# Attention block on one core: how the low halves of the probabilities are shared between VectorE and GpSimd

## The chip, the cores and the metric

One core of a Trainium2 chip runs the whole kernel. The metric is the device time in microseconds (us) of one launch. Engines carry their profile names: PE is TensorE (its matmuls; PEld its weight loads), DVE VectorE, ACT ScalarE, POOL GpSimd, SP the queue that issues the DMAs.

## The reference, cut to what matters

Sixteen images of 32 x 32 positions (1024 tokens) with 512 channels go through group norm, SiLU, one projection to q, k and v, attention with 8 heads of 64 channels, an output projection, a bias and the residual:

```python
xn = jax.nn.silu(group_norm(x, gn_scale, gn_offset))      # x: (16, 32, 32, 512) float32
qkv = jnp.einsum('bxyc,cd->bxyd', xn, w_qkv)
q, k, v = jnp.split(qkv, 3, axis=-1)
...
sim = jnp.einsum('bhdi,bhdj->bhij', q * HEAD_CH ** (-0.5), k)
attn = jax.nn.softmax(sim, axis=-1)
out = jnp.einsum('bhij,bhdj->bhid', attn, v)
out = jnp.einsum('bxyd,dc->bxyc', out, w_out) + b_out
return out + x
```

## The kernel before, in words

Accuracy is kept by splitting each float32 operand into two float16 parts, high and low, and multiplying them in several passes. So every probability exists as `P32` (float32), `Ph` (its float16 high part) and `Pl` (float16 of `P32 - Ph`).

**Units.** Attention of one image is 64 units, written (step, u) with four steps of 16. A unit covers one head, 512 queries and 256 keys. For unit v:

- PE makes the scores in `ST` (two slots, 4 matmuls, lines 1051 and 1052).
- ACT takes the exponential twice: `P32` (line 605, two buffers) and `Ph` (line 608, four buffers, then `exp_done`).
- The low part `Pl = P32 - Ph` is 128 x 1024, cut in two halves: DVE makes columns 0 to 511 (line 812), POOL columns 512 to 1023 (line 495), both as soon as `exp_done` comes.
- Two units later PE multiplies `Ph` and `Pl` with V into `PV` (`times_v`, line 1081). In an even unit that comes right after the scores, in an odd unit at its end.

**Work beside it.** PE also does in each unit a matmul pair into `TP` from which DVE takes the row maxima of scores to come (`mx`, line 759, called max here), and half of a projection job into `SD` (line 949). A job spans an even unit and the odd one after it; at the start of the next even unit ACT writes its high part (not for the "out" jobs) and DVE its low part or result (lines 700, 705, 712), and only then may PE start the next job in `SD`. After every eighth part of the maxima, always in a unit with u % 4 == 1, DVE makes four shifts `ms` (line 729, 128 x 4, inside `top_use` right after the max); PE needs them at the end of that same unit for `TP<-ident,ms` (line 970), and DVE copies that `TP` to `QK2` (line 763) at the start of the next unit, before the job's drain.

**Other side work of DVE and POOL.** For the next image: `turn` (PE transposes x, `("xt", i)`, through an `ST` slot; ACT copies it to `X`), `channel_stats` (bn_stats, line 773), `aggregate`, two chains of tiny operations on 128 x 4 tiles (mean at the start of (1, 0), lines 738 to 744; variance at (1, 4), lines 748 to 755), `newton` on POOL at (1, 5), `coefficients` (DVE, lines 787 to 797, at (1, 7)), and eight `silu` pieces: ACT makes `z` (line 589) and `th` (line 596), DVE multiplies them (line 802, 128 x 512) and casts to float16 (line 805), POOL makes the low part (`low_xn`, line 482). For the output: POOL normalises (`O32`, line 505) after DVE's `sums` (lines 819, 820); `turn` with `("ot", p)` transposes `O32`, ACT copies it, and DVE makes its low part in the next unit (`low_output`, line 721, 128 x 1024); POOL adds the bias (`add_bias`, line 487).

**Order.** Each engine's program is written out by hand: `step` of each engine goes through u = 0 to 15 and looks up in tables of (step, u) what to do after the unit's fixed work. An engine never runs out of this order. Semaphores count; each wait is for a count. The loop holds two images per turn.

Of the kernel before, what the change touches and what calls it, by code (L numbers as in the profile page):

```python
# [10 lines left out]
ALU = mybir.AluOpType  # L11
# [9 lines left out]
HALF = 512  # L21
# [3 lines left out]
UNITS = 64  # L25
# [69 lines left out]
def job_before(step, u, first=False, last=False):  # L95
# [2 lines left out]

TURNS = {(0, 1): ("xt", 0), (0, 3): ("xt", 1), (0, 4): ("ot", 3), (0, 7): ("xt", 2), (0, 9): ("xt", 3),
         (2, 0): ("ot", 0), (2, 8): ("ot", 1), (3, 4): ("ot", 2)}


def unit_turn(step, u, first=False, last=False):
# [11 lines left out]
    return ring  # L117


BN_AT = {(0, 5): (0, 2), (0, 7): (4, 6), (0, 11): (1, 3), (0, 13): (5, 7)}  # L120
AGGREGATE_AT, NEWTON_AT, COEF_AT = (0, 14), (1, 5), (1, 7)
Z_AT = [(1, 8), (1, 11), (1, 13), (2, 1), (2, 4), (2, 7), (2, 11), (2, 13)]
TANH_AT = [(1, 9), (1, 12), (1, 15), (2, 3), (2, 5), (2, 9), (2, 12), (2, 15)]
SILU_AT = [(1, 11), (1, 13), (2, 0), (2, 4), (2, 7), (2, 11), (2, 13), (3, 0)]
LOW_XN_AT = [(1, 12), (1, 14), (2, 1), (2, 5), (2, 8), (2, 12), (2, 14), (3, 1)]
BIAS_AT = {(3, 0): 0, (3, 2): 1, (3, 5): 2, (3, 6): 3}
LATE_BIAS_AT = {(1, 0): 4, (1, 2): 5, (1, 6): 6, (1, 8): 7}


def image_of_tops(b, step, u):  # L130
# [63 lines left out]
def wait(eng, sem, count):  # L194

    if not isinstance(count, int) or count > 0:
        eng.wait_ge(sem, count)


def conv_attention(nc, x, gamma, beta, w_qkv, w_out, b_out, out):  # L200
# [4 lines left out]
    with ctx:  # L205
# [132 lines left out]
        def _(sp):  # L338
# [42 lines left out]
            def step(b, s, cnt, first=False, last=False):  # L381
                for u in range(16):
                    if u % 2 == 0:
                        for use in unit_job(s, u, first, last):
                            cnt.passed(use)
                    if s == 0 and not last:
                        if u == 0 and first:
                            load_x(b + 1, 0)
                        if u in (1, 3, 7):
                            load_x(b + 1, (1, 3, 7).index(u) + 1)  # L390
                    if s == 0 and u == 4:
                        move_v(b)
# [52 lines left out]
        def _(pool):  # L445
# [44 lines left out]
            def low_probs(b, v):  # L490

                pool.wait_ge(exp_done, UNITS * b + v + 1)

                wait(pool, pv_done, UNITS * b + v - 3)
                nc.gpsimd.tensor_tensor(Pl[:, v % 4, HALF:], P32[:, v % 2, HALF:], Ph[:, v % 4, HALF:], ALU.subtract  # L495
                                        ).then_inc(lo_pool, 1)

            def normalise(b, half):
# [11 lines left out]
            def step(b, s, par, first=False, last=False):  # L510
                for u in range(16):
                    v = 16 * s + u
                    if not (first and v == 0):
                        low_probs(b, v - 1)
                    if v % 4 == 3 and not (first and v == 3):
                        normalise(b, v // 4 - 1)
                    if (s, u) == NEWTON_AT and not last:
                        newton(b + 1)
                    if (s, u) in LOW_XN_AT and not last:
                        low_xn(b + 1, 1 - par, LOW_XN_AT.index((s, u)))  # L520
                    if (s, u) in BIAS_AT:
# [30 lines left out]
        def _(act):  # L552
# [46 lines left out]
            def exponentials(b, v, cnt):  # L599
                slot = cnt.next_slot()  # L600
                act.wait_ge(scores_ready, UNITS * b + v + 1)

                wait(act, lo_dve, UNITS * b + v - 1)
                wait(act, lo_pool, UNITS * b + v - 1)
                nc.scalar.activation(P32[:, v % 2, :], ST[:, slot, :], ACT.Exp, scale=cns[:, 0:1])  # L605

                wait(act, pv_done, UNITS * b + v - 3)
                nc.scalar.activation(Ph[:, v % 4, :], ST[:, slot, :], ACT.Exp, scale=cns[:, 0:1]  # L608
                                     ).then_inc(exp_done, 1)
# [60 lines left out]
        def _(dve):  # L670
# [136 lines left out]
            def low_probs(b, v):  # L807

                dve.wait_ge(exp_done, UNITS * b + v + 1)

                wait(dve, pv_done, UNITS * b + v - 3)
                nc.vector.tensor_tensor(Pl[:, v % 4, 0:HALF], P32[:, v % 2, 0:HALF], Ph[:, v % 4, 0:HALF],  # L812
                                        ALU.subtract).then_inc(lo_dve, 1)

            def sums(b, half):

# [6 lines left out]
            def step(b, s, par, cnt, first=False, last=False):  # L823
                turned = []
                for u in range(16):
# [4 lines left out]
                        top_use(use, b + 1, cnt)  # L830
                    for use in job_before(s, u, first, last):
                        side(use, image_of(use, b, s), cnt)
                    for use, slot in turned:
                        low_output(use[1], image_of(use, b, s), slot)
                    if not (first and v == 0):
                        low_probs(b, v - 1)
                    if v % 4 == 3 and not (first and v == 3):
                        sums(b, v // 4 - 1)
                    for use in unit_max(s, u, last):
# [92 lines left out]
            step(B - 2, 3, 0, now)  # L932
            for s in range(4):
                step(B - 1, s, 1, now, last=True)
            low_probs(B - 1, UNITS - 1)
            sums(B - 1, 15)
            low_output(3, B - 1, now.next_slot())
            for t in range(TB):
# [4 lines left out]
        def _(pe):  # L943
# [112 lines left out]
            def times_v(b, v, cnt):  # L1056

                head, kp = v // 8, v % 4
                pe.wait_ge(exp_done, UNITS * b + v + 1)
                if kp == 0:  # L1060

                    wait(pe, pv_out, 16 * b + v // 4)
# [2 lines left out]
                if v == 32:  # L1065
                    pe.wait_ge(v_moved, 16 * (b + 1))
                for i in range(2):
                    pe.wait_ge(lo_pool if i else lo_dve, UNITS * b + v + 1)
                    kb = 2 * kp + i
                    for qb in range(4):  # L1070
                        at, to = i * HALF + qb * P, qb * (LO + HD)
# [107 lines left out]
```

## Time and profile before

| | |
|---|---|
| median of 3 runs | 3912.16 us (3911.99 to 3916.34) |
| the profiled execution | 3913.47 us, its span 3911.7 us |
| PE busy | 3645.2 us, 93% of the span |
| DVE busy | 3350.5 us, 86% |
| ACT busy | 2812.9 us, 72% |
| POOL busy | 1766.6 us, 45% |
| chain that ended last | PE 59%, DVE 24%, issue 12%, ACT 3% |

In the timeline rows, the bracket is the engine's idle time just before the row and what ended it. The busy time of PE is a sum of matmul durations that overlap, so 93% is not a measure of what is left. Steady images follow each other in the middle of the span; image 5's first score matmul starts at 1300.2 us, image 6's at 1535.4 us. Times of the timeline views below are us from the span's start.

### The profile page before, as it was taken

To read this page: it belongs to the slowest core of one execution; us is meant where nothing else is said; L and a number is where in the kernel's file an instruction comes from. 1 tells how busy PE (TensorE), PEld (TensorE's weight loads), DVE (VectorE), ACT (ScalarE), POOL (GpSimd) and SP (SyncE) were. 2 spreads that over 40 slices of the span, in tenths; PEclk is the share of its full clock that TensorE was granted. 3 is DMA by queue.
4 is the path that set the end of the run, shared out by engine and by line. 5 is a ranking of instruction groups with operands and counts; after the bars stand their busy time and mean duration, and the time that the engine had idled before them with its cause. 6 is when DMAs were issued, how large, how long until landed. Compare 5 with 4: busy or idle time off the path is not lost.

```text
span 3911.7 us, 92342 instructions
## 1 busy us (share of the span) xinstructions
PE 3645.2 (93%) x32844; PEld 2099.9 (54%) x32844; DVE 3350.5 (86%) x4368; ACT 2812.9 (72%) x3074; POOL 1766.6 (45%) x1738
## 2 busy tenths in 40 slices
PE   3889999999999999999999999999999999999997
PEld 1455555555555555555555555555555555555553
DVE  5688888988898898988989888898988989888885
ACT  2577677777777777777777777777777777777774
POOL 1244444445445354444445444454444545444443
PEclk7999999999999999999999999999999999999999
DMA  2211212221121321212222121321212222131220
GB/s 77 56 44 51 76 39 66 55 74 52 45 82 34 88 55 45 82 39 66 55 69 58 44 80 36 87 55 45 79 42 66 55 69 58 39 84 37 62 59 33
DMA packets 120727, 228.89 MB, mean 59 GB/s; under 512 B 12624, under 2 KB 29008, under 8 KB 120272
## 3 DMA queue, kind: packets, MB, share of 16 engines
q1 hardware_dynamic: 120272, 222.87, 21.0%
q8 instruction: 279, 4.57, 0.5%
q14 instruction: 176, 1.44, 0.1%
HBM read 71.57 MB, written 33.55 MB: 27 GB/s over the span
## 4 chain that ended last, share of the span: by engine, by line
PE 59%; DVE 24%; issue 12%; ACT 3%; DVEq 1%; DMA 1%; POOL 0%; SPq 0%; ACTq 0%; POOLq 0%
PE SD L949 22%; PE PV L1081 11%; DVE mx L759 8%; PE ST L1051 8%; PE ST L1052 8%; PE TP L963 7%; DVE Pl L812 4%; DVE z L802 3%; DVE ms L729 2%; PE TP L970 2%; PE ST L1016 1%; DVE res L712 1%; PE ST L1023 1%; DVE st L773 1%; DVE OT L721 1%
## 5 line engine op out<-in xcount | busy, mean ns | idle before, releaser
L495 POOL TENSOR_TENSOR Pl<-P,Ph 128x512 f16<-128x512 f32 x1024 | 1240.1, 1211 | 1714.7 <-ACT Ph L608 1705.1
L605 ACT ACTIVATE P<-ST,cns 128x1024 f32<-128x1024 f32 x1024 | 1142.1, 1115 | 896.2 <-PE ST L1052 866.5
L759 DVE TENSOR_REDUCE mx<-TP 128x1 f32<-128x1024 f32 x1024 | 1246.4, 1217 | 165.2 <-PE TP L963 157.4
L608 ACT ACTIVATE Ph<-ST,cns 128x1024 f16<-128x1024 f32 x1024 | 1134.6, 1108 | 0.0
L812 DVE TENSOR_TENSOR Pl<-P,Ph 128x512 f16<-128x512 f32 x1024 | 978.8, 956 | 10.2 <-ACT Ph L608 6.1
L1081 PE MATMUL PV<-V,Ph 128*128 128x129 f16 (+2 forms) x10240 | 862.6, 210 | 4.4 <-POOL Pl L495 1.6
L1081 PEld LDWEIGHTS PV<-V,Ph 128*128 128x128 f16 x10240 | 772.3, 97 | 126.3 <-ACT pv_sum L616 9.2
L1081 PE MATMUL PV<-V,Pl 128*128 128x65 f16 x8192 | 835.2, 192 | 0.0
L1081 PEld LDWEIGHTS PV<-V,Pl 128*128 128x128 f16 x8192 | 723.2, 98 | 108.8 <-issue 0.8
L1051 PE MATMUL ST<-QK 128*128 128x512 f16 x2048 | 778.5, 380 | 0.2 <-ACT Ph L608 0.2
L1052 PE MATMUL ST<-QK 128*128 128x512 f16 x2048 | 778.1, 380 | 0.0
L949 PE MATMUL SD<-X,wq 128*128 128x512 f16 x3072 | 751.4, 381 | 23.6 <-POOL X L482 16.3
L963 PE MATMUL TP<-QK 128*128 128x512 f16 x2048 | 610.7, 380 | 27.1 <-DVE QK L763 14.0
L949 PEld LDWEIGHTS SD<-X,wq 128*128 128x128 f16 x3072 | 293.7, 98 | 406.7 <-DVE QK L700 43.0
L949 PE MATMUL SD<-wo,OT 128*128 128x512 f16 x1536 | 377.1, 383 | 45.5 <-DVE QK L700 28.2
L949 PE MATMUL SD<-wq,X 128*128 128x512 f16 x1536 | 374.3, 381 | 17.0 <-DVE V L705 15.4
L1051 PEld LDWEIGHTS ST<-QK 128*128 128x128 f16 x2048 | 202.9, 99 | 183.7 <-issue 2.5
L1052 PEld LDWEIGHTS ST<-QK 128*128 128x128 f16 x2048 | 200.6, 98 | 182.1 <-issue 2.2
L949 PEld LDWEIGHTS SD<-wo,OT 128*128 128x128 f16 x1536 | 145.9, 98 | 245.8 <-DVE res L712 39.0
L763 DVE CAST QK<-TP 64x512 f16<-64x512 f32 x256 | 176.0, 687 | 116.4 <-PE TP L970 113.7
L700 DVE SCALAR_TENSOR_TENSOR QK<-SD,sc,QK 128x512 f16<-128x512 f32 x256 | 191.4, 748 | 95.8 <-ACT QK L562 80.8
L505 POOL TENSOR_TENSOR O<-pv_sum,den 128x256 f32<-128x256 f32 x256 | 158.1, 617 | 239.0 <-DVE pv_sum L820 237.1
(96 smaller groups left out, 2849.6 us busy)
## 6 DMA issues: line engine op xcount, KB each, us to landing
QK<-QK SPq DMA_DIRECT2D x384, 256.0 KB, 4.7
res<-in_x SPq DMA_DIRECT2D x128, 256.0 KB, 2.8
out<-res SPq DMA_DIRECT2D x128, 256.0 KB, 2.0
x_in<-in_x SPq DMA_DIRECT2D x61, 512.0 KB, 3.8
V<-V SPq DMA_DIRECT2D x16, 1040.0 KB, 6.4
V<-in_L_conv_w_qkv SPq DMA_DIRECT2D x1, 3072.0 KB, 10.7
P<-in_L_conv_w_out SPq DMA_DIRECT2D x1, 1024.0 KB, 12.2
z<-in_x SPq DMA_DIRECT2D x1, 512.0 KB, 6.8
```

The source lines that it names most:

```text
L495: nc.gpsimd.tensor_tensor(Pl[:, v % 4, HALF:], P32[:, v % 2, HALF:], Ph[:, v % 4, HALF:], ALU.subtract).then_inc(lo_pool, 1)
L605: nc.scalar.activation(P32[:, v % 2, :], ST[:, slot, :], ACT.Exp, scale=cns[:, 0:1])
L608: nc.scalar.activation(Ph[:, v % 4, :], ST[:, slot, :], ACT.Exp, scale=cns[:, 0:1]).then_inc(exp_done, 1)
L700: nc.vector.scalar_tensor_tensor(out=QK[:, lo, cols], in0=SD[:], scalar=sc[:, col:col + 1], in1=QK[:, hi, cols], op0=ALU.mult, op1=ALU.sub ...
L759: nc.vector.reduce_max(mx[:, hh, qb:qb + 1], TP[:], AX.X).then_inc(top_drained, 1)
L763: nc.vector.tensor_copy(QK2[r, head_slot(pair, hh), 0, bass.ts(half, HALF)], TP[r, 0:HALF]).then_inc(top_drained, 1)
L812: nc.vector.tensor_tensor(Pl[:, v % 4, 0:HALF], P32[:, v % 2, 0:HALF], Ph[:, v % 4, 0:HALF], ALU.subtract).then_inc(lo_dve, 1)
L949: ins = nc.tensor.matmul(SD[:], stationary(i, c), moving(j, c), start=(c == 0 and i + j == 0), stop=(c == CC - 1 and i == 1))
L963: ins = nc.tensor.matmul(TP[:, bass.ts(kh, HALF)], QK1[:, slot, 0, bass.ts(qb, P)], QK1[:, slot, 1, bass.ts(kh, HALF)], start=True, stop=True)
L1051: nc.tensor.matmul(dst, QK1[:, at, 1, kb], QK1[:, at, 0, bass.ts(q, HALF)], start=True, stop=False)
L1052: ins = nc.tensor.matmul(dst, QK2[:, at, 1, kb], QK2[:, at, 0, bass.ts(q, HALF)], start=False, stop=True)
L1081: ins = nc.tensor.matmul(PV[:, cols], stationary, moving, start=kb == qb == n == 0, stop=kb == TB - 1, skip_group_check=True)
```

## The change

The probabilities' low part is no longer cut in halves. DVE makes it whole (128 x 1024) for even units, POOL whole for odd units. Both still do so while the next unit is being scored: DVE in its odd units, POOL in its even units. The waits follow: the exponential of unit v waits for the low part of unit v - 2 by the engine that makes it, and `times_v` waits once for one engine, ahead of all its matmuls, where it waited for each half. `low_output` comes after the low part on DVE, not before. The tables place side work elsewhere: bn_stats one per unit, SiLU pieces all in odd units, `low_xn` and the bias in even units, the turns of x 2 and 3 at (0, 5) and (0, 7) with their loads to match, the turn of output pair 1 at (2, 12).

```diff
-TURNS = {(0, 1): ("xt", 0), (0, 3): ("xt", 1), (0, 4): ("ot", 3), (0, 7): ("xt", 2), (0, 9): ("xt", 3),
-         (2, 0): ("ot", 0), (2, 8): ("ot", 1), (3, 4): ("ot", 2)}
+TURNS = {(0, 1): ("xt", 0), (0, 3): ("xt", 1), (0, 4): ("ot", 3), (0, 5): ("xt", 2), (0, 7): ("xt", 3),
+         (2, 0): ("ot", 0), (2, 12): ("ot", 1), (3, 4): ("ot", 2)}
...
-SILU_AT = [(1, 11), (1, 13), (2, 0), (2, 4), (2, 7), (2, 11), (2, 13), (3, 0)]
+SILU_AT = [(1, 9), (1, 13), (1, 15), (2, 3), (2, 5), (2, 9), (2, 11), (2, 15)]
...
-LATE_BIAS_AT = {(1, 0): 4, (1, 2): 5, (1, 6): 6, (1, 8): 7}
+LATE_BIAS_AT = {(1, 0): 4, (1, 2): 5, (1, 4): 6, (1, 6): 7}
...
 POOL, low_probs and step:
-                nc.gpsimd.tensor_tensor(Pl[:, v % 4, HALF:], P32[:, v % 2, HALF:], Ph[:, v % 4, HALF:], ALU.subtract
+                nc.gpsimd.tensor_tensor(Pl[:, v % 4, :], P32[:, v % 2, :], Ph[:, v % 4, :], ALU.subtract
                                         ).then_inc(lo_pool, 1)
...
-                    if not (first and v == 0):
+                    if v % 2 == 0 and not (first and v == 0):
                         low_probs(b, v - 1)
...
 ACT, exponentials:
-                wait(act, lo_dve, UNITS * b + v - 1)
-                wait(act, lo_pool, UNITS * b + v - 1)
+                wait(act, lo_pool if v % 2 else lo_dve, 32 * b + v // 2)
...
 DVE, low_probs and step:
-                nc.vector.tensor_tensor(Pl[:, v % 4, 0:HALF], P32[:, v % 2, 0:HALF], Ph[:, v % 4, 0:HALF],
-                                        ALU.subtract).then_inc(lo_dve, 1)
+                nc.vector.tensor_tensor(Pl[:, v % 4, :], P32[:, v % 2, :], Ph[:, v % 4, :], ALU.subtract
+                                        ).then_inc(lo_dve, 1)
...
+                    if v % 2 == 1:
+                        low_probs(b, v - 1)
                     for use, slot in turned:
                         low_output(use[1], image_of(use, b, s), slot)
-                    if not (first and v == 0):
-                        low_probs(b, v - 1)
...
 PE, times_v:
                 pe.wait_ge(exp_done, UNITS * b + v + 1)
+                pe.wait_ge(lo_pool if v % 2 else lo_dve, 32 * b + v // 2 + 1)
...
-                    pe.wait_ge(lo_pool if i else lo_dve, UNITS * b + v + 1)
```

The first place is DVE's order around the output turn of unit (3, 4), rows of register arithmetic left out. Before:

```order
L700 SCALAR_TENSOR_TENSOR QK<-SD,sc,QK 128x512
L812 TENSOR_TENSOR Pl<-P,Ph 128x512
L759 TENSOR_REDUCE mx<-TP 128x1
L721 TENSOR_TENSOR OT<-ST,OT 128x1024
L812 TENSOR_TENSOR Pl<-P,Ph 128x512
L759 TENSOR_REDUCE mx<-TP 128x1
L729 TENSOR_SCALAR ms<-mx,cns 128x4
```

The same place on DVE with the change:

```order
L700 SCALAR_TENSOR_TENSOR QK<-SD,sc,QK 128x512
L759 TENSOR_REDUCE mx<-TP 128x1
L812 TENSOR_TENSOR Pl<-P,Ph 128x1024
L721 TENSOR_TENSOR OT<-ST,OT 128x1024
L759 TENSOR_REDUCE mx<-TP 128x1
L729 TENSOR_SCALAR ms<-mx,cns 128x4
```

Between the max of unit (3, 4) and the one of (3, 5) stood 1024 + 512 columns of work; now 1024 + 1024, with the half ahead of the first max gone.

The second place is DVE's order in units (2, 4) and (2, 5), with the start of (2, 6), around one SiLU piece (`z` and `X`). Before:

```order
L812 TENSOR_TENSOR Pl<-P,Ph 128x512
L759 TENSOR_REDUCE mx<-TP 128x1
L802 SCALAR_TENSOR_TENSOR z<-th,z 128x512
L805 CAST X<-z 128x512
L812 TENSOR_TENSOR Pl<-P,Ph 128x512
L759 TENSOR_REDUCE mx<-TP 128x1
L729 TENSOR_SCALAR ms<-mx,cns 128x4
L763 CAST QK<-TP 64x512
L700 SCALAR_TENSOR_TENSOR QK<-SD,sc,QK 128x512
```

The same units on DVE with the change:

```order
L759 TENSOR_REDUCE mx<-TP 128x1
L812 TENSOR_TENSOR Pl<-P,Ph 128x1024
L759 TENSOR_REDUCE mx<-TP 128x1
L729 TENSOR_SCALAR ms<-mx,cns 128x4
L802 SCALAR_TENSOR_TENSOR z<-th,z 128x512
L805 CAST X<-z 128x512
L763 CAST QK<-TP 64x512
L700 SCALAR_TENSOR_TENSOR QK<-SD,sc,QK 128x512
```

The SiLU piece stood ahead of the shifts `ms`; now it stands behind them, and ahead of the copy of `TP` and the drain of the job.

## Rows read from the trace of the kernel before

**Rows 1.** The page, part 1: busy time and share of each engine.

```profile
PE 3645.2 (93%) x32844; PEld 2099.9 (54%) x32844; DVE 3350.5 (86%) x4368; ACT 2812.9 (72%) x3074; POOL 1766.6 (45%) x1738
```

**Rows 2.** Waits of PE: engine, line, releaser: us in total, times, longest us.

```profile
PE TP L970 <- DVE ms L729: 98.1, 98, 3.0
PE SD L949 <- DVE QK L700: 36.5, 18, 3.4
...
PE SD L949 <- DVE V L705: 15.4, 36, 1.6
PE SD L949 <- DVE res L712: 14.8, 49, 0.8
PE TP L963 <- DVE QK L763: 14.0, 30, 2.1
```

**Rows 3.** Groups by line: busy us, mean ns; then idle before and releasers.

```profile
L495 POOL TENSOR_TENSOR Pl<-P,Ph 128x512 f16<-128x512 f32 x1024 | 1240.1, 1211 | 1714.7 <-ACT Ph L608 1705.1 <-PE PV L1081 6.5 <-POOL gn L476 3.1
L812 DVE TENSOR_TENSOR Pl<-P,Ph 128x512 f16<-128x512 f32 x1024 | 978.8, 956 | 10.2 <-ACT Ph L608 6.1 <-DVE mv L779 2.7 <-issue 0.7
...
L505 POOL TENSOR_TENSOR O<-pv_sum,den 128x256 f32<-128x256 f32 x256 | 158.1, 617 | 239.0 <-DVE pv_sum L820 237.1 <-PE PV L1081 1.9
```

**Rows 4.** Timeline, SiLU piece at (1, 13): start, duration, engine, operation [idle before].

```profile
1409.91 0.69 DVE L802 SCALAR_TENSOR_TENSOR z<-th,z 128x512 f32<-128x512 f32 x1
1410.63 1.26 DVE L805 CAST X<-z 128x512 f16<-128x512 f32 x1
...
1410.18 1.43 POOL L495 TENSOR_TENSOR Pl<-P,Ph 128x512 f16<-128x512 f32 x1 [2.48 <-ACT Ph L608]
...
1412.67 0.61 PE L963 MATMUL TP<-QK 128*128 128x512 f16 x2 [0.41 <-DVE QK L763]
1413.46 1.25 PE L949 MATMUL SD<-wo,OT 128*128 128x512 f16 x5 [0.18 <-DVE res L712]
```

**Rows 5.** Timeline, image 5, end of unit (0, 1).

```profile
1306.85 1.16 POOL L495 TENSOR_TENSOR Pl<-P,Ph 128x512 f16<-128x512 f32 x1 [1.48 <-ACT Ph L608]
1307.14 0.89 DVE L729 TENSOR_SCALAR ms<-mx,cns 128x4 f16<-128x4 f32 x1
1308.09 0.40 PE L970 MATMUL TP<-ident,ms 128*128 128x128 f16 x4 [0.24 <-DVE ms L729]
```

**Rows 6.** Timeline, image 5, units (3, 4) and (3, 5), which hold an output turn.

```profile
1497.15 1.23 DVE L759 TENSOR_REDUCE mx<-TP 128x1 f32<-128x1024 f32 x1 [1.22 <-PE TP L963]
1498.29 1.21 DVE L721 TENSOR_TENSOR OT<-ST,OT 128x1024 f16<-128x1024 f32 x1
...
1500.20 1.21 DVE L759 TENSOR_REDUCE mx<-TP 128x1 f32<-128x1024 f32 x1
1501.44 0.23 DVE L729 TENSOR_SCALAR ms<-mx,cns 128x4 f16<-128x4 f32 x1
...
1501.51 1.18 POOL L495 TENSOR_TENSOR Pl<-P,Ph 128x512 f16<-128x512 f32 x1 [1.78 <-ACT Ph L608]
...
1501.73 0.40 PE L970 MATMUL TP<-ident,ms 128*128 128x128 f16 x4
```

**Rows 7.** The page, part 6: a DMA issue, count, KB each, us to landing.

```profile
x_in<-in_x SPq DMA_DIRECT2D x61, 512.0 KB, 3.8
```

**Rows 8.** Timeline, image 5, unit (2, 5), PE, after a SiLU piece in (2, 4).

```profile
1441.80 0.28 PE L970 MATMUL TP<-ident,ms 128*128 128x128 f16 x2 [1.47 <-DVE ms L729]
```

**Rows 9.** Timeline, image 5, starts of units (1, 0) and (1, 4), DVE and POOL.

```profile
1360.78 1.20 DVE L742 TENSOR_TENSOR gn<-gn 128x4 f32<-128x4 f32 x1
...
1360.69 1.27 POOL L487 TENSOR_TENSOR res<-res,bias 128x512 f32<-128x512 f32 x1
...
1374.11 0.55 DVE L751 TENSOR_SCALAR gn<-gn 128x4 f32<-128x4 f32 x1
...
1373.48 1.16 POOL L495 TENSOR_TENSOR Pl<-P,Ph 128x512 f16<-128x512 f32 x1 [0.75 <-ACT Ph L608]
```

**Rows 10.** Timeline, image 5, unit (1, 8), PE, behind the coefficients of (1, 7).

```profile
1391.74 0.82 PE L949 MATMUL SD<-wo,OT 128*128 128x512 f16 x3 [2.19 <-DVE QK L700]
```

More of the change, by code:

```diff
@@ L117, in ring_of @@
     return ring
-BN_AT = {(0, 5): (0, 2), (0, 7): (4, 6), (0, 11): (1, 3), (0, 13): (5, 7)}
+BN_AT = {(0, 5): (0,), (0, 6): (2,), (0, 7): (4,), (0, 8): (6,), (0, 9): (1,), (0, 10): (3,), (0, 12): (5,),
+         (0, 13): (7,)}
 AGGREGATE_AT, NEWTON_AT, COEF_AT = (0, 14), (1, 5), (1, 7)
-Z_AT = [(1, 8), (1, 11), (1, 13), (2, 1), (2, 4), (2, 7), (2, 11), (2, 13)]
-TANH_AT = [(1, 9), (1, 12), (1, 15), (2, 3), (2, 5), (2, 9), (2, 12), (2, 15)]
-SILU_AT = [(1, 11), (1, 13), (2, 0), (2, 4), (2, 7), (2, 11), (2, 13), (3, 0)]
-LOW_XN_AT = [(1, 12), (1, 14), (2, 1), (2, 5), (2, 8), (2, 12), (2, 14), (3, 1)]
-BIAS_AT = {(3, 0): 0, (3, 2): 1, (3, 5): 2, (3, 6): 3}
-LATE_BIAS_AT = {(1, 0): 4, (1, 2): 5, (1, 6): 6, (1, 8): 7}
+Z_AT = [(1, 7), (1, 9), (1, 12), (1, 15), (2, 3), (2, 5), (2, 8), (2, 11)]
+TANH_AT = [(1, 8), (1, 11), (1, 13), (2, 1), (2, 4), (2, 7), (2, 9), (2, 13)]
+SILU_AT = [(1, 9), (1, 13), (1, 15), (2, 3), (2, 5), (2, 9), (2, 11), (2, 15)]
+LOW_XN_AT = [(1, 10), (1, 14), (2, 0), (2, 4), (2, 6), (2, 10), (2, 12), (3, 0)]
+BIAS_AT = {(3, 2): 0, (3, 6): 1, (3, 8): 2, (3, 10): 3}
+LATE_BIAS_AT = {(1, 0): 4, (1, 2): 5, (1, 4): 6, (1, 6): 7}
 def image_of_tops(b, step, u):
@@ L388, in step @@
                             load_x(b + 1, 0)
-                        if u in (1, 3, 7):
-                            load_x(b + 1, (1, 3, 7).index(u) + 1)
+                        if u in (1, 3, 5):
+                            load_x(b + 1, (1, 3, 5).index(u) + 1)
                     if s == 0 and u == 4:
@@ L934, in _ @@
                 step(B - 1, s, 1, now, last=True)
-            low_probs(B - 1, UNITS - 1)
             sums(B - 1, 15)
```

## The prediction

> **What bounds the kernel now.** The page comes first: PE is busy 93% of the span, DVE 86%, POOL 45% [rows 1]. PE is the engine to keep fed; DVE has little to spare. Next the waits of PE [rows 2]: almost all it loses in the steady part it loses to DVE. The five rows add up to 178.8 us (98.1 + 36.5 + 15.4 + 14.8 + 14.0), about 11.5 us in each of the 15 or 16 images. That is what the change can win at most; the other 3.7 ms is PE's own work and the prologue. More than half is one wait, PE for the four shifts `ms`.
>
> Then the groups and the timelines say why DVE is late. The mean of DVE's half of `Pl` is 956 ns [rows 3]. Where nothing disturbs it the same shape takes 0.68 us: the SiLU product, also 128 x 512 with two inputs from SBUF, took 0.69 us [rows 4]. The rest is waiting for POOL inside the instruction. [Rows 5] show it bare: `ms`, four columns, takes 0.89 us instead of 0.23 us [rows 6] because POOL's `Pl` started 0.29 us ahead of it; it ends at 1308.03, 0.02 us after POOL does. [Rows 4] show it both ways: POOL's `Pl` starts at 1410.18 inside the SiLU product, takes 1.43 instead of 1.16 us, and the cast behind the product, 0.03 us late, lies until 1411.89, 0.28 us after POOL's end at 1411.61. So the one that comes first holds SBUF for its whole instruction, and a waiting POOL instruction slips in between two of DVE. The maxima and the drains read PSUM and do not wait (1.21 to 1.23 us in [rows 6], whatever POOL does).
>
> **Durations after the change.** POOL: 256 columns take 0.617 us [rows 3], 512 take 1.16 [rows 5]; another 512 cost 1.08, so a whole unit takes 2.24 us. DVE: 128 x 1024 took 1.21 us in `OT` [rows 6], and the low part has the same width; two halves cost 2 x 0.956. DVE's busy time thus falls by 512 x (1.91 - 1.21) = 360 us, some 23 us an image, and POOL's hardly moves. But PE waits for DVE only at certain places, so the sum is made there.
>
> The Trainium skill (VectorE: DVE Perf Modes, section on the TRN2 errata) says that operations reading SBUF pay their latency once per instruction, so few large ones beat many small ones. The rows agree on the size (2 x 0.68 - 1.21 = 0.15 us a pair); by that rule alone the sum would be a gain of 512 x 0.15 = 77 us if DVE were the bound, against the loss found below.
>
> **Regular units.** A pair of units takes 235.2 / 32 = 7.3 us on average (images 5 to 6). In it DVE has two maxima, a drain of about 0.7 us and its `Pl`, 2 x 1.22 + 0.7 + 1.21 = 4.4 us; POOL's `Pl` with a bias or `low_xn` behind it (1.27 us in [rows 9]) takes 2.24 + 1.27 = 3.5. The one comes in the odd unit, the other from the odd unit's `exp_done` on, so they miss each other. Nothing is lost, but hardly anything was lost there before. PE reads an odd unit's `Pl` only at the end of the odd unit two later, so POOL's longer instruction is hidden there; likewise ACT's wait for `P32`. The earlier turns of x still stand two units after the one before, 7.3 us, against 3.8 us for their load [rows 7]; `move_v`, queued behind the load, was there before. All at nothing. The price is that whatever of DVE falls behind POOL's start now lies 1.08 us longer. In us per image:
>
> *1. Shifts `ms` behind POOL's start.* In a unit with u % 4 == 1 the shifts come ahead of POOL's `Pl` (in [rows 4] even the product behind them does, by 0.27 us), unless something delays the max. At (0, 1) the turn of x does (it stands between scores and max, and POOL waits only for the scores): `ms` is already blocked [rows 5] and will be for 1.08 us more. At (0, 5) there is now a turn of x too; as [rows 5], 0.24 + 1.08 = 1.3. At (3, 5), [rows 6]: max at 1497.15, now the whole `Pl` (1498.29), `OT` (1499.42), the next max (1500.55), `ms` at 1501.79. POOL starts at 1501.51. Before, `ms` passed it by 0.07 us; now it misses by 0.28 and ends at 1503.78, and PE's `TP` comes at 1503.83 in place of 1501.73: +2.1. Sum 4.5.
>
> *2. The other output turns*, (2, 1) and (2, 13), have the same chain, but the SiLU piece before holds PE and with it POOL's start back by about the missing 0.3 us. Even odds on 2.2 each: 2.2. Bounds 0 and 4.4.
>
> *3. SiLU pieces.* All eight are now in odd units, after the max, so POOL's `Pl` slips in between product and cast as in [rows 4]. There PE lost 0.41 + 0.18 by these rows, which show a matmul's end some 0.15 us late, so 0.9 in all; a cast 1.08 us later makes it 1.9 to 2.0. Four pieces stand where a copy of `TP` follows (u % 4 == 1): 4 x 1.9 = 7.6. Two stand at u % 4 == 3 with no turn after, 1.4 each; two have a turn of about 0.9 us after them, 0.5 each. Sum 11.4. Gone are three pieces in even units, which made the next `ms` late: one costs 1.47 [rows 8], and such places make up most of the 98.1 us, 6.1 per image [rows 2]; gone too are the five old odd pieces, 2.7. So 11.4 - 8.8 = +2.6. Bounds 0 (POOL's start falls behind the cast) and 5.
>
> *4. Tiny operations.* At (1, 0) `L742` already waits for POOL's bias [rows 9]; both POOL instructions now hold it to 1.1 us later. The max behind it comes too late for the next `TP` (0.7), and the shifts of (1, 1) then fall behind POOL's `Pl` (1.5): 2.2. At (1, 4) `L751` waits for the end of `Pl` [rows 9], now 1.1 us later, and the bias now placed at (1, 4) may take a further 1.2 in front of the next two; the drain and PE's `SD` wait for them: 1.7. At (1, 7) ACT's first `z` now stands ahead of unit 8's high part and waits for the coefficients; its 0.8 us and what hangs on it add 1.0 to the 2.19 of [rows 10]. Sum 4.9, bounds 2 and 7.
>
> *5. Gone with the smoother order*: one turn of x at (0, 9), bn_stats in pairs, small drains: -1.2.
>
> Sum 4.5 + 2.2 + 2.6 + 4.9 - 1.2 = **+13.0 us an image**. Side work for a next image runs 15 times: 195 us. The profiled execution took 3913.5 us (1.3 above the median), so 3913.5 + 195 = 4108.
>
> **Rivals.** *A (0.13): DVE is the real bound, and the change is faster.* For it: DVE's 86% and its 24% of the chain, and the 360 us of DVE time that go. It decides if casts and shifts mostly find POOL off SBUF, so that terms 1 to 4 vanish and half to all of the 178.8 us goes: 3735 to 3825, say 3815. Against it: [rows 4] is the very order that all eight pieces get.
>
> *B (0.15): POOL's longer instruction lets DVE in midway.* No row shows a POOL instruction above 512 columns on SBUF from which DVE's wait could be read. Then the blocked ones lose no more than today; left are +1.0 at (3, 5), about 1 at (2, 1) and (2, 13), +1 at (1, 8), 2 in term 3: +4 an image, 3975. The Trainium skill (SBUF — State Buffer, section "two separate sides") speaks against B: the pair of ports is locked for the full instruction.
>
> *C (0.04): it is hidden.* Gains of even SiLU pieces (6.1) cancel the losses: 3910.
>
> **How the numbers follow.** My forecast has 0.68. Its own bounds: terms at their low ends give +4, at their high ends +20, 3975 to 4210. About 0.2% is what a measurement can tell from no change. Faster is A, 0.13; same is C, 0.04; slower is the forecast and B, 0.83. The range takes in B and most of the forecast's bounds and leaves A out: 3930 to 4190.
>
> **What would show it.** Right: POOL's `Pl` at 2.24 us, DVE's at 1.21 and mostly undisturbed; `ms` of over 2 us at (0, 1), (0, 5) and (3, 5); casts `X<-z` at about 2.3 us in all odd units; PE's wait for `ms`, `QK` L763 and the drains up from 179 to some 370 us; DVE's busy time down all the same, by less than 360. Wrong: if `ms` stays near 0.23 us in the (3, 5) units, or the casts at 0.43 us, or if PE's waits for DVE shrink.

## The result, and the profile after

The changed kernel takes **4165.66 us** (median of 4 runs, 4164.22 to 4167.66); the kernel before, run beside it, takes 3913.01 us. The ratio is 1.0644, with a 95% interval of 1.0626 to 1.0663: 253 us slower. The forecast was 4108 us, 195 us slower.

The page of the changed kernel, part 1 and the first line of part 4, answering to [rows 1]:

```profile
PE 3696.1 (89%) x32844; PEld 2112.8 (51%) x32844; DVE 3303.4 (79%) x3856; ACT 2819.4 (68%) x3074; POOL 1619.4 (39%) x1226
...
PE 45%; issue 22%; DVE 14%; POOL 7%; ACT 5%; DMA 1%; DVEq 0%; POOLq 0%; SPq 0%; ACTq 0%
```

Every engine but PE is busy for less time or the same, and the kernel is slower. That is what a loss by waiting looks like. POOL now stands in the chain with 7%; before, it had 0%.

The waits of PE, answering to [rows 2] (us in total, times, longest):

```profile
PE TP L969 <- DVE ms L729: 162.3, 86, 2.9
PE SD L948 <- DVE QK L700: 84.5, 48, 3.1
PE TP L962 <- DVE QK L763: 77.7, 59, 2.1
PE SD L948 <- DVE V L705: 22.1, 21, 1.6
PE ST L1015 <- DVE OT L721: 19.9, 14, 1.4
...
PE SD L948 <- DVE res L712: 8.4, 21, 0.8
```

The five waits that made 178.8 us before make 355.0 now (162.3 + 84.5 + 77.7 + 22.1 + 8.4), 176 more. A wait of 19.9 us, the turn of x behind the output's low part, is new. PE's busy time grew by 51 us at the same number of matmuls, most of it because part of them ran at a lower granted clock (below). 176 + 20 + 51 = 247 of the 250.7 us by which the span grew. Busy and waiting time can be added up here: the page counts matmuls that overlap only once, so PE's busy and idle time make up the span (3645.2 + 266.5 before, 3696.1 + 466.3 after). The text ahead of the prediction takes the 93% for a sum of overlapping durations, which it is not.

The 250.7 us are spread over the images: image 5 to image 6 is 1379.05 to 1630.95 us, 251.9 in place of 235.2; the mean of images 3 to 12 grew by 16.2 us, and the last image, which prepares no next one, still by 11.

The groups, answering to [rows 3]:

```profile
L496 POOL TENSOR_TENSOR Pl<-P,Ph 128x1024 f16<-128x1024 f32 x512 | 1101.1, 2151 | 1427.6 <-ACT Ph L608 1426.2 <-issue 1.2
L812 DVE TENSOR_TENSOR Pl<-P,Ph 128x1024 f16<-128x1024 f32 x512 | 623.0, 1217 | 15.7 <-ACT Ph L608 9.3 <-DVE mv L779 2.7 <-issue 1.9
```

The same groups before and after for the two operations that pay; before:

```profile
L729 DVE TENSOR_SCALAR ms<-mx,cns 128x4 f16<-128x4 f32 x256 | 116.3, 454 | 9.1
...
L805 DVE CAST X<-z 128x512 f16<-128x512 f32 x128 | 115.9, 906 | 4.4
```

after:

```profile
L805 DVE CAST X<-z 128x512 f16<-128x512 f32 x128 | 264.5, 2066 | 4.4
...
L729 DVE TENSOR_SCALAR ms<-mx,cns 128x4 f16<-128x4 f32 x256 | 198.1, 774 | 9.1
```

DVE saved 978.8 - 623.0 = 356 us on `Pl`, as counted. But the casts and the shifts took back 149 + 82 of it as waiting inside the instruction, the statistics more, and its busy time fell by 47 us only.

Unit (3, 4) to (3, 5) of image 5, the place of [rows 6] (timeline: start, duration, engine, operation, idle before):

```profile
1591.82 1.22 DVE L812 TENSOR_TENSOR Pl<-P,Ph 128x1024 f16<-128x1024 f32 x1
1592.95 1.22 DVE L721 TENSOR_TENSOR OT<-ST,OT 128x1024 f16<-128x1024 f32 x1
1594.09 1.21 DVE L759 TENSOR_REDUCE mx<-TP 128x1 f32<-128x1024 f32 x1
1595.34 1.84 DVE L729 TENSOR_SCALAR ms<-mx,cns 128x4 f16<-128x4 f32 x1
...
1595.04 2.12 POOL L496 TENSOR_TENSOR Pl<-P,Ph 128x1024 f16<-128x1024 f32 x1 [5.33 <-ACT Ph L608]
...
1597.24 0.40 PE L969 MATMUL TP<-ident,ms 128*128 128x128 f16 x4 [2.00 <-DVE ms L729]
```

`ms` missed POOL's start by 0.30 us (forecast: 0.28), lay until 1597.18, 0.02 us after POOL's end, and PE idled 2.00 us. Unit (1, 13) to (1, 14), the place of [rows 4]:

```profile
1497.41 0.68 DVE L802 SCALAR_TENSOR_TENSOR z<-th,z 128x512 f32<-128x512 f32 x1
1498.13 2.24 DVE L805 CAST X<-z 128x512 f16<-128x512 f32 x1
...
1497.78 2.30 POOL L496 TENSOR_TENSOR Pl<-P,Ph 128x1024 f16<-128x1024 f32 x1 [4.47 <-ACT Ph L608]
...
1501.15 0.60 PE L962 MATMUL TP<-QK 128*128 128x512 f16 x2 [1.37 <-DVE QK L763]
```

The cast takes 2.24 us (forecast: about 2.3) and PE's copy of `TP` comes late.

### The profile page after: what moved, and what is told of

Read it like the earlier page. It is cut to its first block, busy times and chain, and to the rows that moved or that the text cites. A ratio compares the mean times of both kernels' runs of the same rounds, so it can differ in the third digit from the quotient of the medians.

```text
span 4162.4 us, 89409 instructions
## 1 busy us (share of the span) xinstructions
PE 3696.1 (89%) x32844; PEld 2112.8 (51%) x32844; DVE 3303.4 (79%) x3856; ACT 2819.4 (68%) x3074; POOL 1619.4 (39%) x1226
## 4 chain that ended last, share of the span: by engine, by line
PE 45%; issue 22%; DVE 14%; POOL 7%; ACT 5%; DMA 1%; DVEq 0%; POOLq 0%; SPq 0%; ACTq 0%
PE SD L948 17%; PE PV L1080 8%; PE TP L962 6%; PE ST L1051 6%; PE ST L1050 6%; POOL Pl L496 4%; DVE mx L759 4%; DVE ms L729 3%; ACT Ph L608 2%; DVE OT L721 2%; ACT OT L583 1%; PE ST L1015 1%; PE TP L969 1%; POOL res L488 1%; DMA QK<-QK 1%
## 5 line engine op out<-in xcount | busy, mean ns | idle before, releaser
L496 POOL TENSOR_TENSOR Pl<-P,Ph 128x1024 f16<-128x1024 f32 x512 | 1101.1, 2151 | 1427.6 <-ACT Ph L608 1426.2
L962 PE MATMUL TP<-QK 128*128 128x512 f16 x2048 | 619.0, 384 | 91.7 <-DVE QK L763 77.7
L812 DVE TENSOR_TENSOR Pl<-P,Ph 128x1024 f16<-128x1024 f32 x512 | 623.0, 1217 | 15.7 <-ACT Ph L608 9.3
L948 PE MATMUL SD<-wo,OT 128*128 128x512 f16 x1536 | 386.1, 390 | 48.7 <-DVE QK L700 37.8
L962 PEld LDWEIGHTS TP<-QK 128*128 128x128 f16 x2048 | 163.1, 98 | 219.5 <-DVE QK L763 45.5
```

The source lines that it names most:

```text
L496: nc.gpsimd.tensor_tensor(Pl[:, v % 4, :], P32[:, v % 2, :], Ph[:, v % 4, :], ALU.subtract).then_inc(lo_pool, 1)
L812: nc.vector.tensor_tensor(Pl[:, v % 4, :], P32[:, v % 2, :], Ph[:, v % 4, :], ALU.subtract).then_inc(lo_dve, 1)
L948: ins = nc.tensor.matmul(SD[:], stationary(i, c), moving(j, c), start=(c == 0 and i + j == 0), stop=(c == CC - 1 and i == 1))
L962: ins = nc.tensor.matmul(TP[:, bass.ts(kh, HALF)], QK1[:, slot, 0, bass.ts(qb, P)], QK1[:, slot, 1, bass.ts(kh, HALF)], start=True, stop=True)
```

## The terms, unit by unit

The mean time from one unit's first score matmul to the next unit's, over images 3 to 12, in us. An undisturbed unit with u % 4 == 1 takes 3.5, any other undisturbed one 3.3, with a turn 4.17.

| unit | before | after | what is in it |
|---|---|---|---|
| (0, 1) | 4.81 | 5.78 | `ms` behind POOL's start, both times |
| (0, 5) | 3.55 | 6.04 | a turn of x moved in (0.9), and 1.6 of waiting |
| (3, 5) | 3.71 | 5.70 | `ms` behind POOL's start, now |
| (2, 1) | 4.84 | 5.74 | before: SiLU piece in (2, 0); now `ms` blocked |
| (2, 13) | 3.62 | 5.70 | `ms` blocked |
| (1, 1) | 3.61 | 5.70 | `ms` blocked, behind the mean's tiny operations |
| (1, 4) | 3.43 | 5.14 | the variance's tiny operations |
| (1, 8) + (1, 9) | 9.17 | 11.35 | the coefficients and ACT's first `z` |
| (1, 10), (1, 14) | 3.30, 4.23 | 4.90, 5.20 | after a SiLU piece, (1, 14) both times |
| (2, 2), (2, 14) | 3.30, 4.23 | 3.96, 3.79 | now 4.95 in the images in which PE's clock falls there, 3.30 in the others |

## The experiments

All are measured against 3911 to 3914 us for the kernel before, run on the same chip beside them. Each but the last is one execution, so a few us between two of them say nothing. The savings are against the 4165.66 us of the changed kernel.

**Turns and loads moved to even units** (`e1_turns`). The changed kernel with this alone:

```diff
-TURNS = {(0, 1): ("xt", 0), (0, 3): ("xt", 1), (0, 4): ("ot", 3), (0, 5): ("xt", 2), (0, 7): ("xt", 3),
-         (2, 0): ("ot", 0), (2, 12): ("ot", 1), (3, 4): ("ot", 2)}
+TURNS = {(0, 0): ("xt", 0), (0, 2): ("xt", 1), (0, 4): ("xt", 2), (0, 6): ("ot", 3), (0, 8): ("xt", 3),
+         (2, 2): ("ot", 0), (2, 6): ("ot", 1), (3, 6): ("ot", 2)}
-BN_AT = {(0, 5): (0,), (0, 6): (2,), (0, 7): (4,), (0, 8): (6,), (0, 9): (1,), (0, 10): (3,), (0, 12): (5,),
-         (0, 13): (7,)}
+BN_AT = {(0, 3): (0, 2), (0, 5): (4,), (0, 9): (6,), (0, 11): (1, 3), (0, 12): (5,), (0, 13): (7,)}
-                        if u in (1, 3, 5):
+                        if u in (0, 2, 4):
```

> The changed kernel with all turns moved so that none stands in or ahead of a unit with shifts in an odd place: x turns at (0, 0), (0, 2), (0, 4), (0, 8), output turns at (0, 6), (2, 2), (2, 6), (3, 6), loads and bn_stats to match. Theory (shifts fall behind POOL's whole-unit low part): the waits for ms at (0, 1), (0, 5), (2, 1), (2, 13) and (3, 5), about 9.6 us an image, go: 4166 - 150 = about 4015 us. Rival (DVE's longer instruction alone makes it late, wherever the turns stand): about 4166, at most 30 us less.

Measured: 4026.61 us, 139 less than the changed kernel. The wait for `ms`:

```profile
PE TP L968 <- DVE ms L728: 48.9, 26, 3.1
```

From 162.3 to 48.9 us, and from 86 times to 26: four of the five places per image are gone, the fifth, (1, 1), has no turn. So at these four what makes `ms` late is the turn ahead of it, and each wait was worth 113.4 / 60 = 1.9 us. The 19.9 us of the turn of x behind the output's low part are gone too.

**SiLU pieces where POOL is off SBUF** (`e2_silus`). The pieces go to the start of an odd unit with u % 4 == 3, ahead of the max (one, at (2, 13), stays behind the max):

```diff
-SILU_AT = [(1, 9), (1, 13), (1, 15), (2, 3), (2, 5), (2, 9), (2, 11), (2, 15)]
+SILU_AT = [(1, 11), (1, 15), (2, 3), (2, 7), (2, 11), (2, 13), (2, 15), (3, 3)]
...
+                    if (s, u) in SILU_AT and u % 4 == 3 and not last:
+                        silu(b + 1, 1 - par, SILU_AT.index((s, u)))
```

(`Z_AT`, `TANH_AT` and `LOW_XN_AT` move along; the first `z` is at (1, 8) instead of (1, 7), and `low_xn` follows in the same odd unit, but for the piece at (2, 13).)

> The changed kernel with seven SiLU pieces in units with u % 4 == 3 ahead of the max, where POOL is off SBUF, and one left at (2, 13). Theory: product and cast take 0.68 and 0.43 us there and PE's waits behind them, about 9.4 us an image, shrink to about 2: 4166 - 110 = about 4055 us. Rival (the SiLU piece costs PE its own 1.1 us of DVE wherever it stands): within 30 us of 4166.

Measured: 3986.06 us, 180 less than the changed kernel, and 69 less than expected. The cast's group:

```profile
L805 DVE CAST X<-z 128x512 f16<-128x512 f32 x128 | 85.8, 671 | 4.4
```

It takes 671 ns on average in place of 2066. That is not quite undisturbed: seven of the eight casts take 0.72 us, 0.3 of it behind POOL's short `O` instruction (line 506), and the one after (2, 13) takes 0.43. The 180 us are 12.0 an image. Most of what comes on top of the expected gain is not the pieces': units (1, 8) and (1, 9) take 4.55 + 3.52 = 8.07 us in place of 11.35, since ACT's first `z` no longer waits for the coefficients at (1, 7). That leaves 12.0 - 3.3 = 8.7 us for the eight pieces.

**Statistics moved** (`e3_stats`). The mean's tiny operations after the max of (1, 2), the variance's after that of (1, 4), the coefficients at (1, 6), one late bias piece elsewhere:

```diff
-AGGREGATE_AT, NEWTON_AT, COEF_AT = (0, 14), (1, 5), (1, 7)
+AGGREGATE_AT, NEWTON_AT, COEF_AT = (0, 14), (1, 5), (1, 6)
-LATE_BIAS_AT = {(1, 0): 4, (1, 2): 5, (1, 4): 6, (1, 6): 7}
+LATE_BIAS_AT = {(1, 0): 4, (1, 2): 5, (1, 4): 6, (1, 8): 7}
...
+                        if (s, u) == (1, 2):
+                            mean_rest()
+                        if (s, u) == (1, 4):
+                            var_rest()
```

> The changed kernel with the tiny operations of mean and variance put off until after the max of (1, 2) and (1, 4), and the coefficients at (1, 6). Theory: the waits at (1, 0), (1, 1), (1, 4), (1, 8) and (1, 9), about 8.5 us an image with the slower PE clock after the long one, go: 4166 - 120 = about 4045 us, and the granted clock stays at 1.00 in steady images. Rival (tiny operations cost their dependent latencies, not POOL's lock): no more than 30 us less.

Measured: 4049.77 us, 116 less. Thus thirteen operations on 128 x 4 (of fifteen; the two that read PSUM stayed), with what waits for them, cost 7.7 us an image where they stood. Some 3.3 of it is ACT's first `z`, below, which finds its coefficients ready here.

**POOL's low part in two instructions** (`e4_pooltwo`) **and in four** (`e9_poolfour`). Nothing else is changed: same tables, same share, same order.

```diff
-                nc.gpsimd.tensor_tensor(Pl[:, v % 4, :], P32[:, v % 2, :], Ph[:, v % 4, :], ALU.subtract
-                                        ).then_inc(lo_pool, 1)
+                for i in range(4):
+                    cols = bass.ts(i, HALF // 2)
+                    part = nc.gpsimd.tensor_tensor(Pl[:, v % 4, cols], P32[:, v % 2, cols], Ph[:, v % 4, cols],
+                                                   ALU.subtract)
+                part.then_inc(lo_pool, 1)
```

> The changed kernel with POOL's whole-unit low part issued as two instructions of 512 columns back to back. Theory (SBUF is held for one instruction, whatever its length): a waiting DVE instruction gets in between the two, blocked ms and casts end about 1.1 us earlier, 12 to 14 places an image: about 3985 us. Rival (the POOL queue keeps SBUF from instruction to instruction, or DVE is late for its own length): 4166 or slightly more, as POOL gets 0.1 us longer.

> The changed kernel with POOL's whole-unit low part in four instructions of 256 columns, tables of the change. Theory (a DVE instruction waits for the one POOL instruction under way): from one piece to two each blocked ms or cast came about 1.0 us earlier, 4166 to 3954 us; from two to four it comes about 0.5 us earlier again where PE still waits: 3850 to 3890 us, though POOL is 0.3 us longer per unit. Rival (what two pieces gained was a lucky alignment): 3954 us or more.

Measured: 3954.36 us with two (some 30 less than expected), 3887.11 with four (as expected), against 4165.66 with one. The same `ms` of unit (3, 5) that took 1.84 us above, in the kernel with two:

```profile
1511.33 1.15 POOL L496 TENSOR_TENSOR Pl<-P,Ph 128x512 f16<-128x512 f32 x1 [5.19 <-ACT Ph L610]
1511.63 0.87 DVE L731 TENSOR_SCALAR ms<-mx,cns 128x4 f16<-128x4 f32 x1
1512.44 1.15 POOL L498 TENSOR_TENSOR Pl<-P,Ph 128x512 f16<-128x512 f32 x1
...
1512.57 0.40 PE L971 MATMUL TP<-ident,ms 128*128 128x128 f16 x4 [1.04 <-DVE ms L731]
```

and with four (the first row merges three of the four pieces):

```profile
1483.95 1.92 POOL L498 TENSOR_TENSOR Pl<-P,Ph 128x256 f16<-128x256 f32 x3 [4.90 <-ACT Ph L611]
1484.25 0.39 DVE L732 TENSOR_SCALAR ms<-mx,cns 128x4 f16<-128x4 f32 x1
...
1484.70 0.40 PE L972 MATMUL TP<-ident,ms 128*128 128x128 f16 x4 [0.55 <-DVE ms L732]
```

`ms` starts 0.30 us behind POOL's start in all three, and ends when POOL's first instruction does: 1.84, 0.87, 0.39 us. PE waits 2.00, 1.04, 0.55. So SBUF is held for one instruction, not for the whole series, and a waiting DVE instruction gets in between two POOL instructions that stand back to back. That settles the cause: POOL's work even grew (1619.4 to 1858.1 us busy), and the kernel is 278 us faster. What is left is small: 3887.11 is 25 us above the 3861.76 of the halves with the same tables (`e6_newtables`, next). It agrees with the Trainium skill (SBUF — State Buffer, section "two separate sides"), by which the pair of ports is held for the whole instruction.

**Whole units with the old tables** (`e5_oldtables`) **and halves with the new tables** (`e6_newtables`). The two parts of the change, each alone: the first takes `low_probs`, its waits and its order from the change and all tables and the load units from the kernel before; the second the reverse. The first differs from the change by its tables, of which these two show the manner; the second by the halves, which come back as they stand with a minus in the diff of the change:

```diff
-SILU_AT = [(1, 9), (1, 13), (1, 15), (2, 3), (2, 5), (2, 9), (2, 11), (2, 15)]
+SILU_AT = [(1, 11), (1, 13), (2, 0), (2, 4), (2, 7), (2, 11), (2, 13), (3, 0)]
-BIAS_AT = {(3, 2): 0, (3, 6): 1, (3, 8): 2, (3, 10): 3}
+BIAS_AT = {(3, 0): 0, (3, 2): 1, (3, 5): 2, (3, 6): 3}
```

> The changed kernel (whole units by turns, low part ahead of the output's low part on DVE) with all tables of the kernel before. Theory (the loss is the length for which POOL now holds SBUF; the tables only choose where it strikes): the SiLU pieces in even units, the turns at (0, 9) and (2, 8) and the chain at (1, 0) lose as much as the new places do: 4130 to 4190 us. Rival (the loss comes from the new tables): near 3913 us.

> The kernel before (halves, POOL holds SBUF for 1.16 us) with all tables of the change. Theory: near the kernel before, 3900 to 3960 us; shifts and casts blocked at the same places, but for 1.1 us less each; the first z at (1, 7) still costs some 2 us an image. Rival (the tables are the loss): above 4050 us.

| | tables of before | tables of the change |
|---|---|---|
| halves | 3913 | 3861.76 |
| whole units | 4206.31 | 4166 |

The first came out a little above what was expected, the second well below. Whole units cost 293 us in the one column and 304 in the other; the tables gain 51 and 40. The wait for `ms` in the kernel with whole units and old tables, and then in the one with halves and new tables:

```profile
PE TP L968 <- DVE ms L728: 265.4, 143, 3.1
```

```profile
PE TP L971 <- DVE ms L730: 24.1, 27, 3.0
```

That the tables are a gain by themselves was expected neither here nor in the prediction. With halves, the SiLU pieces behind the max in odd units make their casts wait for a 1.16 us instruction, and free `ms` (98.1 us of waiting before, 24.1 now).

**ACT's first `z` one unit later** (`e11b_firstz`). The changed kernel with this alone:

```diff
-Z_AT = [(1, 7), (1, 9), (1, 12), (1, 15), (2, 3), (2, 5), (2, 8), (2, 11)]
+Z_AT = [(1, 8), (1, 9), (1, 12), (1, 15), (2, 3), (2, 5), (2, 8), (2, 11)]
```

(and in each unit ACT makes `z` ahead of `th`, since both fall in (1, 8).)

> The changed kernel with ACT's first z piece at (1, 8), behind the job's high part and the exponentials and ahead of the first th piece, instead of (1, 7). Theory (the first z waits for the coefficients and holds up the high part that PE's next job waits for; the long wait then costs PE its faster clock for a while): units (1, 8) and (1, 9) take 8.1 to 8.5 us together instead of 11.35 and the granted clock there stays at 1.00: 4166 - 48 = about 4118 us. Rival (DVE's coefficients are the wait, whoever needs them): within 15 us of 4166.

Measured: 4118.25 us, 47 less. The windows view over units (1, 8) and (1, 9) of image 5 (us, busy time and count of each engine, PEclk, DMA share, GB/s), in this kernel:

```profile
1456.61:1464.67 8.06, 6.98 (x69) 3.89 (x67) 7.39 (x10) 6.43 (x8) 2.34 (x2) 1.00 0.43 89
```

in the changed kernel, with its two units apart and together:

```profile
1471.60:1478.47 6.87, 4.17 (x36) 1.95 (x34) 5.17 (x7) 4.10 (x5) 2.10 (x1) 0.90 0.11 23
1478.47:1482.97 4.50, 4.50 (x35) 2.34 (x34) 2.40 (x4) 2.56 (x3) 0.36 (x1) 0.78 0.94 210
1471.60:1482.97 11.37, 8.67 (x69) 4.29 (x67) 7.57 (x10) 6.65 (x8) 2.46 (x2) 0.85 0.44 97
```

The same 69 matmuls are busy for 8.67 us in place of 6.98, at a granted clock of 0.85 in place of 1.00. So 3.3 us hang on one ACT instruction per image, 1.7 of them by the clock.

**All three placements together** (`e7_all3`), **and with POOL's low part in two** (`e8_all3two`). Edits as in the first three experiments, and as above.

> The changed kernel with the moves of e1, e2 and e3 together: turns, SiLU pieces and statistics all placed where POOL is off SBUF. Theory: what is left is PE's own 221 us an image, some 2 us behind the one SiLU piece left at (2, 13) and some 1.5 us of small waits: 4166 - 27 x 15.5 = about 3750 us, faster than both kernels. Rival (DVE at its limit; the three gains overlap): above 3850 us.

> e7 with POOL's low part in two instructions. Theory: only the piece at (2, 13) still falls behind POOL, so at most 1 us an image less, 15 us, against POOL's 0.1 us more: 3735 to 3755 us.

Measured: 3798.26 and 3777.62 us, 48 and some 30 more than expected. The three alone add up to 139 + 180 + 116 = 435 us, of which about 50 (3.3 an image) are counted twice, since both the second and the third clear (1, 8): 385 against the measured 367. Most of the rest is (2, 14): the one piece left behind the max, at (2, 13), still has its cast blocked (2.24 us) and costs 1.9 us an image there, where the second experiment alone lost less. Another 0.7 each are left at (2, 4) and (2, 8), behind units that hold both an output's low part and a SiLU piece. Splitting POOL's instruction now gains 21 us where it gained 211 before the moves: the two remedies pay for the same waits.

**Halves with the moved tables** (`e10_halves_all3`, and again, timed in five runs, as `e12_halves_timed`). The kernel before's halves, waits and order of `low_probs`, with the turns, pieces and statistics of the three experiments. Against the three placements together:

```diff
-                nc.gpsimd.tensor_tensor(Pl[:, v % 4, :], P32[:, v % 2, :], Ph[:, v % 4, :], ALU.subtract
+                nc.gpsimd.tensor_tensor(Pl[:, v % 4, HALF:], P32[:, v % 2, HALF:], Ph[:, v % 4, HALF:], ALU.subtract
                                         ).then_inc(lo_pool, 1)
...
-                    if v % 2 == 0 and not (first and v == 0):
+                    if not (first and v == 0):
                         low_probs(b, v - 1)
```

> The kernel before, each low part in halves on both engines, with the tables of the change and the moves of e1, e2 and e3. Theory: with the side work placed off POOL, halves lose only what each half waits for the other, which the order absorbs: 3770 to 3820 us, about as e7 (3798). Rival (whole units by turns are needed for these places to work): above 3850 us, near e6 (3862).

> The kernel of e10 again, timed: 3750 to 3756 us, 4% faster than the kernel before.

Measured: 3752.56 us in one run, below the range expected; **3754.51 us** as the median of 5 runs (3752.22 to 3756.24), with 3913.77 before. The ratio to the kernel before is 0.9595, interval 0.9582 to 0.9609. Its page and its wait for `ms`:

```profile
PE 3610.9 (96%) x32844; PEld 2098.6 (56%) x32844; DVE 3223.5 (86%) x4368; ACT 2813.6 (75%) x3074; POOL 1756.0 (47%) x1738
```

```profile
PE TP L988 <- DVE ms L729: 14.6, 10, 2.5
```

It beats both kernels, and it beats the best one with whole units, by 44 us (by 23 that with two POOL instructions). DVE is busy 290 us more than in the whole-unit kernel with the same placement (2933.8 us) and the kernel is faster: DVE's busy time was not the bound.

## Why the prediction was right and where it was wrong

**The direction, the mechanism and most places were right.** The one that comes first holds SBUF, and what falls behind POOL's start lies as much longer as POOL's instruction is longer. POOL's `Pl` took 2.13 us (2.24 forecast), DVE's 1.22 (1.21), the casts 2.07 on average, 2.2 to 2.4 where they are blocked (2.3). The five waits of PE were to reach some 370 us and reached 355. Two signs failed in size: `ms` was to take over 2 us at (0, 1), (0, 5) and (3, 5) and took 1.86, 0.23 and 1.84, and POOL's busy time, which was hardly to move, fell by 147 us.

**Rival A** (DVE the real bound, 3815) fell. DVE's busy time did go down and the time went up; the halves beat the whole units at every set of tables. The rule on few large operations that was weighed there (the Trainium skill, VectorE: DVE Perf Modes, section on the TRN2 errata) holds for the size: 1217 ns against 2 x 0.68 us. But it speaks of one engine by itself; here the 77 us that it promises stand beside a loss of 293 to 304.

**Rival B** (DVE gets in midway, 3975) fell: the rows with one, two and four pieces show each wait ending with a POOL instruction, never inside one. **Rival C** (hidden, 3910) fell with the result.

**The terms**, in us per image; the measured ones come from the unit table:

| step | forecast | measured |
|---|---|---|
| 1 shifts behind POOL's start | 4.5 | 4.6 |
| 2 the other output turns | 2.2 | 4.4 |
| 3 SiLU pieces | +2.6 | about +1.0 |
| 4 tiny operations | 4.9 | 6.0 |
| 5 gone with the smoother order | -1.2 | -1.4 |
| not in the prediction: small losses, mostly PE's clock | 0 | +1.7 |
| sum | +13.0 | +16.2 |

*Step 1* was right in sum, but at (0, 5) by another way. There `ms` was not blocked:

```profile
1400.95 1.22 DVE L721 TENSOR_TENSOR OT<-ST,OT 128x1024 f16<-128x1024 f32 x1
...
1405.04 0.23 DVE L729 TENSOR_SCALAR ms<-mx,cns 128x4 f16<-128x4 f32 x1
```

PE's turn of x at (0, 5) waited 1.4 us for the low part of the output turned at (0, 4), which DVE now makes after its whole `Pl`; this is the new row of 19.9 us. POOL started as always, 3.3 us into the unit, and `ms` came so late that POOL was all but done:

```profile
1402.22 1.09 PE L1015 MATMUL ST<-ident,x_in 128*128 128x128 f32 x8 [1.42 <-DVE OT L721]
...
1403.03 2.13 POOL L496 TENSOR_TENSOR Pl<-P,Ph 128x1024 f16<-128x1024 f32 x1 [6.21 <-ACT Ph L608]
```

The prediction saw that the two turns now stand in neighbouring units and did not follow the slot from one to the other. That its 1.3 is near the measured 1.6 at (0, 5) is luck: either way `ms` ends at about POOL's end.

*Step 2 is the largest mistake.* It gave even odds to (2, 1) and (2, 13), because a SiLU piece ahead would hold POOL's start back by the missing 0.3 us. Both take 5.7 us on the mean of ten images, against 3.5 undisturbed: 2.2 each. The piece did hold PE and POOL back, by about 0.23 us, which was not enough: `ms` missed POOL's start by 0.05 to 0.07 us there, against 0.30 at (3, 5), and lost all the same. At (2, 1) of image 5:

```profile
1514.20 2.12 POOL L496 TENSOR_TENSOR Pl<-P,Ph 128x1024 f16<-128x1024 f32 x1 [4.05 <-ACT Ph L608]
...
1514.27 2.08 DVE L729 TENSOR_SCALAR ms<-mx,cns 128x4 f16<-128x4 f32 x1
```

The upper bound, 4.4, was the right value.

*Step 3* was sized too high. It charged 11.4 us to the eight pieces; the eight units that follow one take 37.65 us together, less 8 x 3.3 and two turns of 0.87 in them 9.5, and the second experiment gives 8.7. What they replaced was forecast at 8.8 and is some 8.5 by the same count (1.2 of it at (2, 9), behind the old output turn of (2, 8) and not a piece).

*Step 4*: (1, 1) 2.1 (2.2 forecast) and (1, 4) 1.7 (1.7) are as worked out. (1, 8) + (1, 9) lost 2.2, not 1.0. The step saw that ACT's first `z` waits for the coefficients ahead of the high part; the wait grew by 0.5 us only (2.19 to 2.70), and the 1.7 that PE's lower clock costs there was not in the step. Without it the pair takes 8.06 us, 1.1 less than before, so this one entry of a table cost 3.3 an image, 47 us in all by its own run.

*Step 5* was right in size: (0, 9), its turn left out, (0, 14), (0, 6), (1, 2) and some smaller ones gained 1.4 together. What the prediction had nothing for is +1.7 of new small losses. 1.15 of it is at (2, 2) and (2, 14), the units after a blocked `ms`: these take 4.95 us in the images in which PE's clock falls there and 3.30 in the others (last section).

Together 2.2 + 1.1 + 1.7 too little and 1.6 too much, less 0.2 of gain in step 5, make the 3.2 us an image that are missing in images 3 to 12, some 46 us over the 15 images. The last image's 11 us come on top: the prediction counted 15 images, but the last one has shifts and output turns too. Since these errors partly cancel, the sum is nearer to the result than its terms are. Its lower bound was added up wrong as well: the terms at their low ends give 4.5 + 0 + 0 + 2 - 1.2 = +5.3, not +4.

What the prediction didn't ask is whether the two halves of the change have the same sign. They don't: the tables gain 40 to 51 us and whole units lose 293 to 304.

## What to carry to other kernels

Between two engines that exclude each other, the length of one instruction is the price that the other pays for coming second, however small its own work; so keep the instructions of the engine with slack short, even if that engine's busy time grows. Then ask of each operation that reads and writes SBUF which engine comes first there, and move it to a place where the other is off: that was worth 160 us here with the halves left as they were, while cutting the instruction count on DVE lost 293. A change made of a new split and new tables should be costed as two changes, since one can hide the gain of the other.

## What was not expected of the hardware

*The hold is per instruction, with a fine grain.* POOL's two-input float32 subtraction takes 2.13 us for 1024 columns, 1.15 for 512 and 0.67 for 256, and DVE's four-column operation behind it scales with that (1.84, 0.87, 0.39 us). A series of four hides almost all of it.

*A late coefficient lowered PE's clock.* In the changed kernel, PE at (1, 7) and after:

```profile
1471.60 0.38 PE L1050 MATMUL ST<-QK 128*128 128x512 f16 x1
1471.81 0.38 PE L1051 MATMUL ST<-QK 128*128 128x512 f16 x1
...
1476.46 2.21 PE L948 MATMUL SD<-wo,OT 128*128 128x512 f16 x6 [2.70 <-DVE QK L700]
1478.46 0.63 PE L1050 MATMUL ST<-QK 128*128 128x512 f16 x1
1478.89 0.63 PE L1051 MATMUL ST<-QK 128*128 128x512 f16 x1
```

Matmuls of 512 columns follow each other every 0.21 us before (2.4 GHz) and every 0.43 us after (1.2 GHz), behind an idle time of 2.70 us. The granted clock of (1, 9) is 0.78 here and 0.75 and 0.70 one and two images later; over (1, 8) and (1, 9) together it is 0.85 in all three, and the clock falls there in each of images 1 to 14. With the first `z` moved, PE waits 1.08 us there and the clock stays at 1.00 in all of them. So a wait can cost more than its length.

The length of the wait alone does not decide it. Before, the same place waited 1.8 to 2.2 us (2.19 in [rows 10]), and the clock stayed up in all but two of these 14 images. Images 3 and 9 of the kernel before, over (1, 8) and (1, 9), with waits of 2.19 and 2.18 us:

```profile
916.60:925.78 9.18, 6.99 (x70) 3.90 (x68) 7.72 (x14) 5.76 (x7) 3.79 (x5) 1.00 0.38 79
2328.42:2339.27 10.85, 8.67 (x70) 4.32 (x68) 7.73 (x14) 5.77 (x7) 3.77 (x5) 0.84 0.46 103
```

And in the changed kernel (2, 2) runs at the lower clock for a part in 6 of the 14 images, (2, 14) in 3, behind the waits of 2.0 to 2.1 us for `ms`. Unit (2, 2) of images 4 and 5:

```profile
1264.39:1269.33 4.94, 4.94 (x33) 2.65 (x31) 3.28 (x4) 2.12 (x2) 0.00 (x0) 0.65 0.02 3
1516.64:1519.94 3.30, 3.30 (x34) 1.88 (x31) 2.54 (x3) 2.12 (x2) 0.00 (x0) 1.00 0.00 0
```

Each fall costs about 1.7 us. Why it comes in one image and not in the next is not shown; no run lengthened a wait alone.
